# Cross-attention and spectral feed-forward on one core: GpSimd's and ScalarE's work of slots 7 to 12 in another order

## The chip, the cores and the metric

The kernel runs on one core of a Trainium2 chip. The metric is the device time of one execution in microseconds; three executions of the kernel before gave 442.58, 441.76 and 442.54. One further execution was recorded by the hardware profiler, and all rows below come from it.

The engines are TensorE (PE in the profile; PEld is its weight loads), VectorE (DVE), ScalarE (ACT), GpSimd (POOL) and the SP queue (SPq), which issues nearly all transfers. Every engine works through its own list of instructions in order, and they hand work to each other by semaphores.

## What is computed

Two residual layers on x (2 x 2048 rows of 512). This is the reference, cut to what matters:

```python
x = x + cross_attention(layernorm(x), ctx, mask)     # 16 heads of 32, 128 keys
x = x + real(ifft(fft(layernorm(x)) @ w)) + bias     # y = layernorm(x) @ M + bias

score = (q . k) / sqrt(32) * mask
score = where(score == 0, -1e9, score)               # the zero test
context = softmax(score) @ v ;  out = context @ wo + bo
```

## The kernel before

The 4096 rows are 16 blocks of 256 rows (c = 0 to 15), each of two tiles of 128 rows (t = 0, 1). Each block has four attention steps s = 4c to 4c + 3, one for four heads. `plan()` writes one order of slots v = 2 to 79 for all engines; every engine's program is a loop over v with what it has to do in that slot, written out by hand. Nothing is scheduled at run time: a wait at the head of an engine's list holds all behind it.

In slot v TensorE does: `turn` (L616) of step v - 2, 8 transposes of the exponentials in `zs`; a product of the middle kind (`WO` of block c - 2, tile 0 or 1, in slots 4c and 4c + 1; `FF` of block c - 3, tile 0 or 1, in slots 4c + 2 and 4c + 3; in slots 4 to 11 the eight products `U` and `M` that build the matrix M from the spectral weights); the scores of step v + 1 (L590); in odd slots `weigh` (L629), the weighted sum of values; then late products (`R`, `ST`, `QQ`). So WO(0, 0) is in slot 8, WO(0, 1) in 9, FF(0, 0) in 14, FF(0, 1) in 15, just ahead of the scores of step 16, the first step of block 4.

VectorE per step: `mask_mul` (L929), `zero_to_neg` (L936, the zero test), `least` (L941, the row minimum). GpSimd's `bias` (L1189) scales the minimum, and ScalarE's `exps` (L729) needs that. ScalarE's `copy_pt` (L738) copies the turned exponentials, which `weigh` needs; its `high_m` (L708) rounds a row block of M to 16 bits, VectorE's `low_m` (L920) makes the rest of it.

GpSimd also adds the output bias to the rows of x (`add_bo`, L1142), which the WO result is added to; makes the statistics' columns of a block (`stat_cols`, L1116, six small instructions); subtracts for the low half of the context (`ctx_lo`, L1202); spreads reciprocals (`spread`, L1196). From slot 4 on it waits in each slot for `eq_done`, that is until the zero test of that slot's step has ended, ahead of its long work.

After WO(c, t) the rows x1 are split into two 16-bit parts, `x1nh` (`norm_hi2`, L1154 on GpSimd for a few tiles, L716 on ScalarE for the others) and `x1nl` (`norm_lo2`, L1160, on GpSimd, which counts `p_l2`). The SP queue then turns both by DMA (`turn_x1n`, L372: two transposes, L385) into `x1h` and `x1l`, and FF(c, t) on TensorE waits for both (`d_t2`, L583). The order in which the SP queue issues, with its waits, is:

- slot 7: the query stack of block 3, then in slot 8 the mask and transposed rows of later blocks
- slot 11: `turn_x1n(0, 0)` (waits for `p_l2` of 1), `load_x(7)`, `stack_q(4)` (2 transfers of a row and 12 of `qh` and `ql`, L306: the operands of the scores of step 16)
- slot 12: `turn_x1n(0, 1)` (waits for `p_l2` of 2), `load_mask(5)`, `load_xt(7)`
- slot 15: `turn_x1n(1, 0)`, and so on

Per block there is only this one list, so block 0's second pair of transposes is behind the whole query stack of block 4.

Of the kernel before, what the change touches and what calls it, by code (L numbers as in the profile page):

```python
# [17 lines left out]
NC = NB * S // CH  # L18
NS = 4 * NC
# [98 lines left out]

def bo_slot(c):

    return c + 7 if c < 2 else 10 if c == 2 else 4 * c + 3 if c < 13 else 2 * c + 27


def build(nc, x, xt, ctx_in, mask, wq, bq, wk, bk, wv, bv, wo, bo, lparts, tables, bf, eye, sums, pick, places, heads, out):
# [3 lines left out]
    with ExitStack() as stack:  # L128
# [155 lines left out]
        def tile_of(c, t):  # L284
            return 2 * c + t

        def cast_count(n):

            return n + 1 - min(max(n + 1 - tile_of(12, 0), 0), 4)

        def columns(n):

# [370 lines left out]
        def _(act):  # L663
# [42 lines left out]
            def high_m(c):  # L706
                act.wait_ge(g_free, at["M", c] + 1)
                act.activation(mh[:, c, :], mf[:], ACT.Identity, scale=SO / D).then_inc(m_hi, 1)  # L708
# [82 lines left out]
            for v in range(V0, V1):  # L791
                c, r = divmod(v, 4)
                prompt, held, mids = slots[v][1:]
                if v % 2 == 1 and 0 <= v - 5 < NS - 2:
                    copy_rec((v - 5) // 2)
                for n in prompt:
                    hi(n)
                if v == 3:
                    hi(at["QQ", 2, 0])
                if 2 <= v - 1 < NS:  # L800
                    exps(v - 1, 0)
                if 3 < v < VQ:
                    for n in held:
                        hi(n)
                if 0 <= v - 2 < NS:
                    copy_pt(v - 2, 0)
                    copy_pt(v - 2, 1)
                if v == 2:
                    hi(at["ST", 2])
                    act.wait_ge(d_wo, 16)  # L810
                    act.activation(wos[:], wos[:], ACT.Identity, scale=SO).then_inc(w_sc, 1)
                    act.wait_ge(w_sc, 1)
                    act.copy(woh[:], wos[:]).then_inc(w_hi, 1)
                if v == 9:
                    high_m(0)
                if 2 <= v - 1 < NS:
                    exps(v - 1, 1)
                if v % 2 == 1 and 0 <= v - 5 < NS - 2:
                    ctx_hi((v - 5) // 2)
                if v == NS + 1:  # L820
                    copy_rec(NS // 2 - 1)
                if 1 <= v - 9 < 4:
                    high_m(v - 9)
                if v >= VQ:
                    for n in held:
                        hi(n)
                for n in mids:
                    if fills[n] != ("ST", 2):
                        hi(n)
                if v == 3:  # L830
                    split_hi(3)
                if r == 1 and 0 <= c - 2 < NC and v != NS + 1 and c - 2 not in (12, 13):
                    norm_hi2(c - 2, 0)
                if v == NS + 2:
                    norm_hi2(NC - 2, 0)
                    ctx_hi(NS // 2 - 1)
                if v == NS + 3:
                    norm_hi2(NC - 2, 1)
                if r == 2 and 0 <= c - 2 < NC and v != NS + 2 and c - 2 not in (12, 13):
                    norm_hi2(c - 2, 1)  # L840
                for a in range(4, NC):
                    if hi_slot(a) == v:
                        split_hi(a)
# [264 lines left out]
        def _(pool):  # L1108
# [45 lines left out]
            def norm_hi2(c, t):  # L1154
                n = tile_of(c, t)
                pool.wait_ge(g_free, at["WO", c, t] + 1)
                pool.wait_ge(d_t2[t], 32 * c)
                step(pool.tensor_copy(x1nh[:, t], x1[:, n % NO, :]))

            def norm_lo2(c, t):  # L1160
                n = tile_of(c, t)
                if c not in (12, 13):
                    pool.wait_ge(h2_done, cast_count(n))
                pool.tensor_tensor(x1nl[:, t], x1[:, n % NO, :], x1nh[:, t], ALU.subtract).then_inc(p_l2, 1)  # L1164

# [103 lines left out]
            for v in range(V0, V1):  # L1269
                c, r = divmod(v, 4)  # L1270
                if v == 8:
                    constant_row()
                for a in range(5, NC):
                    if small_slot(a) == v:
                        stat_cols(a)
                if v == NS + 1:
                    spread(NS // 2 - 1)
                if r == 1 and 0 <= c - 2 < NC and v != NS + 1:
                    rstd2(c - 2, 0)
                if v == NS + 2:  # L1280
                    rstd2(NC - 2, 0)
                    ctx_lo(NS // 2 - 1)
                if v == NS + 3:
                    rstd2(NC - 2, 1)
                if r == 2 and 0 <= c - 2 < NC and v != NS + 2:
                    rstd2(c - 2, 1)
                if VP <= v < NS:
                    pool.wait_ge(eq_done, v + 1)
                if v in (11, 12):
                    norm_lo2(0, v - 11)  # L1290
                if VT <= v < NS and r >= 2:
                    norm_lo2(c - 2, r - 2)
                if v == 4:
                    split_lo(3, slice(2, 4))
                if v == 5:
                    fold(9)
                if v == 6:
                    ctx_lo(0)
                for a in range(5, NC):
                    if v == 4 * a - 11:  # L1300
                        split_lo(a, slice(0, 2), False)
                    if v == 4 * a - 10:
                        split_lo(a, slice(2, 4))
                for a in range(3, 14):
                    if bo_slot(a) == v:
                        add_bo(a, 0)
                if v == 52:
                    add_bo(12, 1)
                if v == 56:
                    add_bo(13, 1)  # L1310
                if v == 60:
                    add_bo(14, 0)
                if v in (57, 61):
                    norm_hi2(c - 2, 0)
                if 0 <= v < NS:
                    bias(v)
                for n in {2: (4, 5), 4: (6, 7, 8), 5: (10, 11)}.get(v, ()):
                    fold(n)
                if v == 6:
                    split_lo(4)  # L1320
                    stat_cols(4)
                if v == 7:
                    scale_mask(2)
                if v == 9:
                    pool.wait_ge(m_lo, 1)
                if v == 10:
                    pool.wait_ge(m_lo, 2)
                if v % 2 == 1 and 2 <= v - 5 < NS - 2:
                    ctx_lo((v - 5) // 2)
                if r == 2 and 1 <= c - 2 < NC - 1 and not VT <= v < NS:  # L1330
                    norm_lo2(c - 2, 0)
                if r == 3 and 1 <= c - 2 < NC - 1 and not VT <= v < NS:
                    norm_lo2(c - 2, 1)
                if r < 2 and 0 <= c - 3 < NC and v > 12 and not (r == 1 and VT <= v < NS):
                    add_bf(c - 3, r)
                if r == 2 and VT <= v < NS:
                    add_bf(c - 3, 1)
                if v in (58, 62):
                    norm_hi2(c - 2, 1)
                if v == 60:  # L1340
                    add_bo(14, 1)
                if v == 3:
                    low_o(0)
                    spread(0)
                    low_o(1)
                if v == NS + 1:
                    add_bo(15, 0)
                if v == NS + 3:
                    add_bo(15, 1)
                if v == small_slot(3):  # L1350
                    stat_cols(3)
                for a in range(3):
                    if bo_slot(a) == v:
                        add_bo(a, 0)
                        add_bo(a, 1)
                for a in range(3, 12):
                    if bo_slot(a) == v:
                        add_bo(a, 1, slice(0, D // 2), False)
                    if bo_slot(a) + 3 == v:
                        add_bo(a, 1, slice(D // 2, D))  # L1360
                if v == 3:
                    split_lo(3, slice(0, 2), False)
                if v > VP and v % 2 == 1 and 0 <= v - 3 < NS - 2:
                    spread((v - 3) // 2)
                if r == 0 and 3 <= c + 1 < NC:
                    if v == 12:
                        add_bf(0, 0)
                    scale_mask(c + 1)

# [97 lines left out]
```

## Time and profile before

| what | value |
|---|---|
| median of the three runs | 442.54 us |
| the profiled execution | 441.81 us |
| its span, first to last instruction | 439.9 us |
| TensorE busy | 430.4 us, 98% |
| VectorE busy | 398.3 us, 91% |
| ScalarE busy | 366.1 us, 83% |
| GpSimd busy | 357.6 us, 81% |

Busy shares are means over a start-up of about 40 us, a regular middle part and an end; where the time goes is read from the order of the instructions on TensorE and from the idle time ahead of each. A number in square brackets at the end of a row of the timeline is the idle time just ahead of that row, and what ended it.

### The profile page before, as it was taken

The page shows a single profiled execution, that of the slowest core. Times are in us where ns is not written, and L with a number is a line of the kernel's source. Part 1 is how long each engine was busy: PE and PEld are TensorE (multiplying, and loading weights), DVE is VectorE, ACT ScalarE, POOL GpSimd, SP SyncE. Part 2 cuts the span into 40 slices and gives each one's busy share as a digit, 9 for nine tenths or more (in the row PEclk, how much of TensorE's full clock was granted, in tenths as well). Part 3 has the DMA queues.
Part 4 walks back from the last instruction along what each step waited for, and adds up shares of the span by engine and source line. Part 5 has one row for each costly group of instructions (what it writes and reads, how often), then busy time and mean ns, then how long its engine had stood idle before and what let it go on. Part 6 is the DMA issues. An engine that isn't in the chain of part 4 may idle for free.

```text
span 439.9 us, 10908 instructions
## 1 busy us (share of the span) xinstructions
PE 430.4 (98%) x3496; PEld 297.0 (68%) x3496; DVE 398.3 (91%) x532; ACT 366.1 (83%) x1338; POOL 357.6 (81%) x487
## 2 busy tenths in 40 slices
PE   7999999999999999999999999999999999999997
PEld 6887788676666776667677667766667675555544
DVE  2899899999999999999999999999999899999453
ACT  1668998899999899898989998999999899999710
POOL 5879889967979898989989898989898866676782
DMA  8999854404555455535455554455442334321144
GB/s 270 396 390 236 289 180 115 114 0 103 116 136 128 140 97 131 146 110 145 119 149 129 132 149 113 106 100 149 133 101 63 95 89 111 77 73 48 50 107 133
DMA packets 85286, 60.15 MB, mean 137 GB/s; under 512 B 40141, under 2 KB 72813, under 8 KB 84718
## 3 DMA queue, kind: packets, MB, share of 16 engines
q1 hardware_dynamic: 84508, 59.29, 49.6%
q8 instruction: 29, 0.48, 0.5%
q10 hardware_dynamic: 722, 0.17, 0.2%
q14 instruction: 27, 0.22, 0.2%
HBM read 29.33 MB, written 8.39 MB: 86 GB/s over the span
## 4 chain that ended last, share of the span: by engine, by line
PE 81%; DVE 9%; issue 3%; ACT 3%; POOL 3%; DVEq 0%; POOLq 0%
PE bank L467 31%; PE bank L472 22%; PE bank L626 10%; PE bank L640 6%; PE scores L612 5%; PE bank L573 2%; DVE zs L936 2%; PE bank L554 2%; DVE zs L929 2%; ACT zs L729 2%; PE scores L472 1%; PE bank L646 1%; ACT pt L738 1%; POOL cl L1202 1%; DVE cn L954 1%
## 5 line engine op out<-in xcount | busy, mean ns | idle before, releaser
L729 ACT ACTIVATE zs<-zs,nbias 128x128 f32<-128x128 f32 x512 | 199.6, 395 | 11.9 <-POOL nbias L1189 11.3
L729 ACT ACTIVATION_READ_ACCUMULATOR zs<-zs,nbias 128x1 f32 x512 | 98.6, 193 | 0.0
L936 DVE SCALAR_TENSOR_TENSOR zs<-zs 128x1024 f32<-128x1024 f32 x64 | 89.1, 1392 | 1.1
L941 DVE TENSOR_REDUCE nmin<-zs 128x8 f32<-128x1024 f32 x64 | 78.0, 1219 | 2.1
L929 DVE TENSOR_TENSOR zs<-scores,ms 128x1024 f32<-128x1024 f32 x64 | 78.0, 1218 | 0.1
L738 ACT COPY pt<-bank 128x512 f32<-128x512 f32 x128 | 67.8, 581 | 8.0 <-PE bank L626 7.9
L626 PE MATMUL bank<-ident,zs 128*128 128x128 f32 x512 | 67.1, 274 | 1.5 <-ACT zs L729 1.1
L1142 POOL TENSOR_TENSOR xs<-xs,bob 128x512 f32<-128x512 f32 (+1 forms) x41 | 42.3, 1036 | 24.9 <-DVE zs L936 23.5
L472 PE MATMUL bank<-xth,wqh 128*128 128x256 f16 x224 | 61.2, 273 | 0.0
L626 PEld LDWEIGHTS bank<-ident,zs 128*128 128x128 f32 x512 | 57.4, 140 | 5.4 <-ACT zs L729 4.3
L472 PE MATMUL bank<-xth,wql 128*128 128x256 f16 x224 | 61.1, 273 | 0.0
L472 PE MATMUL bank<-xtl,wqh 128*128 128x256 f16 x224 | 61.1, 273 | 0.0
L467 PE MATMUL bank<-woh,ch 128*128 128x512 f16 x128 | 48.5, 379 | 1.4 <-POOL cl L1202 1.4
L467 PE MATMUL bank<-woh,cl 128*128 128x512 f16 x128 | 48.5, 379 | 0.0
L467 PE MATMUL bank<-wol,ch 128*128 128x512 f16 x128 | 48.5, 379 | 0.0
L467 PE MATMUL bank<-mh,x1h 128*128 128x512 f16 x120 | 45.5, 379 | 0.0
L467 PE MATMUL bank<-ml,x1h 128*128 128x512 f16 x120 | 45.5, 379 | 0.0
L467 PE MATMUL bank<-mh,x1l 128*128 128x512 f16 x120 | 45.5, 379 | 0.0
L1196 POOL COPY rzb<-rz 128x512 f32<-128x512 f32 x32 | 41.6, 1299 | 3.8 <-DVE rz L947 3.7
L1164 POOL TENSOR_TENSOR x1nl<-x,x1nh 128x512 f16<-128x512 f32 x30 | 34.8, 1161 | 10.3 <-DVE zs L936 10.3
L612 PEld LDWEIGHTS scores<-ks,qs 102*128 102x128 f16 (+1 forms) x480 | 31.7, 98 | 14.6 <-DVE zs L929 1.6
L1175 POOL TENSOR_TENSOR x<-x,bfb 128x512 f32<-128x512 f32 x32 | 40.8, 1275 | 0.0
(126 smaller groups left out, 903.3 us busy)
## 6 DMA issues: line engine op xcount, KB each, us to landing
xs<-in_x SPq DMA_DIRECT2D x16, 512.0 KB, 4.4
xtr<-in_xt SPq DMA_DIRECT2D x16, 512.0 KB, 4.5
out<-x SPq DMA_DIRECT2D x31, 256.0 KB, 2.5
qs<-qh SPq DMA_DIRECT2D x120, 64.0 KB
lp<-in_lparts SPq DMA_DIRECT2D x4, 1024.0 KB, 10.5
qs<-ql SPq DMA_DIRECT2D x60, 64.0 KB
ms<-in_mask SPq DMA_DIRECT2D x16, 128.0 KB, 2.4
wks<-in_wk SPq DMA_DIRECT2D x2, 512.0 KB, 6.5
```

The source lines that it names most:

```text
L467: last = pe.matmul(o, a, b, start=(i == 0), stop=(i == len(mm) - 1))
L472: last = pe.matmul(o, a, b, start=(first and i == 0), stop=(i == len(pairs) - 1))
L612: last = pe.matmul(A[:, n % 2, 128 * j:128 * j + 128], qs[c % 2][0:rows, g, j, 128 * t:128 * t + 128], ks[0:rows, g, j, c // (NC // NB), : ...
L626: last = pe.transpose(PB[f][:, a:a + 128], zs[:, s % NZ, t, 2 * f + i, :], ident[:])
L729: last = act.activation(z, z, ACT.Exp, bias=nbias[:, s % 4, i:i + 1], scale=-NEG, accum_out=zsum[:, s % 4, i:i + 1])
L738: act.copy(pt[:, s % 2, 2 * f:2 * f + 2, :], PB[f][:]).then_inc(pt_copied, 1)
L929: dve.tensor_tensor(zs[:, s % NZ], A[:].rearrange("p t (h k) -> p t h k", h=4), ms[:, c % NM].unsqueeze(2).broadcast_to([128, 2, 4, KEYS]) ...
L936: dve.scalar_tensor_tensor(out=z, in0=z, scalar=0.0, in1=z, op0=ALU.is_equal, op1=ALU.subtract).then_inc(eq_done, 1)
L941: dve.tensor_reduce(nmin[:, s % 4, :], zs[:, s % NZ].rearrange("p t h k -> p (t h) k"), AX.X, ALU.min).then_inc(mn_done, 1)
L1142: i = pool.tensor_tensor(z, z, bob[:, n], ALU.add)
L1175: pool.tensor_tensor(z, z, bfb[:], ALU.add).then_inc(p_x1b, 1)
L1196: pool.tensor_copy(rzb[:].rearrange("p i h w -> p (i h) w"), rz[:, z, :].rearrange("p i h -> p (i h)").unsqueeze(2).broadcast_to([128, 16, ...
```

## The change

Only GpSimd's and ScalarE's lists change; the lists of TensorE, VectorE and the SP queue are the same instruction for instruction. In words:

- `add_bo` of block 0 leaves slot 7 for slot 8, behind the wait for the zero test of step 8 (its first half ahead of `bias(8)`, its second behind). `add_bo` of block 1 is split over slots 8 and 10, that of block 2 over slots 11 and 14. `stat_cols(5)` comes behind `bias(8)`.
- The high halves of block 0's rows are cast on GpSimd (in slots 9 and 10) and no longer on ScalarE. The low halves, `norm_lo2(0, 0)` and `norm_lo2(0, 1)`, which were in slots 11 and 12 ahead of `bias(11)` and `bias(12)`, both stand at the end of slot 12's list.
- In slot 11 GpSimd also waits for `m_lo` of 3 behind `bias(11)`.
- ScalarE takes the first exponentials of step 8 in slot 8, those of steps 9 and 10 at the head of slots 10 and 11, the second ones of step 9 ahead of `copy_pt`, and the matrix rows (`high_m`) 1, 2 and 3 earlier in their slots.

The core of the diff, ScalarE's loop first:

```diff
+                if v in (10, 11):
+                    exps(v - 1, 0)
...
-                if 2 <= v - 1 < NS:
+                if 2 <= v - 1 < NS and v not in (9, 10, 11):
                     exps(v - 1, 0)
+                if v == 10:
+                    exps(v - 1, 1)
+                    high_m(1)
+                if v == 12:
+                    high_m(3)
...
-                if 2 <= v - 1 < NS:
+                if v == 11:
+                    high_m(2)
+                    hi(at["M", 3])
+                if 2 <= v - 1 < NS and v != 10:
                     exps(v - 1, 1)
+                if v == 8:
+                    exps(v, 0)
...
-                if 1 <= v - 9 < 4:
-                    high_m(v - 9)
...
-                if r == 1 and 0 <= c - 2 < NC and v != NS + 1 and c - 2 not in (12, 13):
+                if r == 1 and 0 <= c - 2 < NC and v != NS + 1 and c - 2 not in (0, 12, 13):
                     norm_hi2(c - 2, 0)
```

GpSimd's loop:

```diff
-                if v in (11, 12):
-                    norm_lo2(0, v - 11)
+                if v == 8:
+                    add_bo(0, 0)
...
+                if v == 8:
+                    add_bo(0, 1)
+                    stat_cols(5)
+                    add_bo(1, 0)
                 if v == 9:
                     pool.wait_ge(m_lo, 1)
+                    norm_hi2(0, 0)
                 if v == 10:
                     pool.wait_ge(m_lo, 2)
+                    norm_hi2(0, 1)
+                    add_bo(1, 1)
+                if v == 11:
+                    pool.wait_ge(m_lo, 3)
...
                     if v == 12:
+                        norm_lo2(0, 0)
+                        norm_lo2(0, 1)
                         add_bf(0, 0)
                     scale_mask(c + 1)
```

GpSimd's order from slot 7 to the middle of slot 8, before. The names: `cl` is the low context, `xs` the rows that get the output bias, `rzb` the spread reciprocals, `ve` to `rs` the start of the statistics' columns, `nbias` the scaled minimum of step 8 behind its wait for the zero test.

```order
L1202 TENSOR_TENSOR cl<-cn,ch 128x512
L1142 TENSOR_TENSOR xs<-xs,bob 128x512 x2
L1196 COPY rzb<-rz 128x512
L1226 MEMSET tb 1x256
L1119 TENSOR_SCALAR ve_98<-ag_97 128x2
L1122 TENSOR_TENSOR rs_99<-ve_98,half 128x2
```

The same place after the change:

```order
L1213 TENSOR_TENSOR cl<-cn,ch 128x512
L1207 COPY rzb<-rz 128x512
L1237 MEMSET tb 1x256
L1152 TENSOR_TENSOR xs<-xs,bob 128x512
L1200 TENSOR_SCALAR nbias<-nmin 128x8
L1152 TENSOR_TENSOR xs<-xs,bob 128x512
```

The two additions to `xs` moved from ahead of the zero test of step 8 to behind it.

GpSimd's order over slots 11 and 12, before, from `norm_lo2(0, 0)` (the first row) to `norm_lo2(0, 1)` (the row ahead of the last); the statistics' columns in the middle are those of block 6, and the last row is `bias(12)`.

```order
L1164 TENSOR_TENSOR x1nl<-x_76,x1nh 128x512
L1189 TENSOR_SCALAR nbias<-nmin 128x8
L1202 TENSOR_TENSOR cl<-cn,ch 128x512
L1196 COPY rzb<-rz 128x512
L1119 TENSOR_SCALAR ve_98<-ag_97 128x2
L1122 TENSOR_TENSOR rs_99<-ve_98,half 128x2
L1123 TENSOR_TENSOR ag_97<-ve_98,half 128x2
L1124 CAST h_100<-ag_97 128x4
L1128 COPY stok<-h_100 128x2x2x2
L1129 TENSOR_TENSOR stok<-ag_97,h_100 128x2x2
L1164 TENSOR_TENSOR x1nl<-x_76,x1nh 128x512
L1189 TENSOR_SCALAR nbias<-nmin 128x8
```

After the change, from `bias(11)` on:

```order
L1200 TENSOR_SCALAR nbias<-nmin 128x8
L1213 TENSOR_TENSOR cl<-cn,ch 128x512
L1152 TENSOR_TENSOR xs<-xs,bob 128x256
L1207 COPY rzb<-rz 128x512
L1129 TENSOR_SCALAR ve_98<-ag_97 128x2
L1132 TENSOR_TENSOR rs_99<-ve_98,half 128x2
L1133 TENSOR_TENSOR ag_97<-ve_98,half 128x2
L1134 CAST h_100<-ag_97 128x4
L1138 COPY stok<-h_100 128x2x2x2
L1139 TENSOR_TENSOR stok<-ag_97,h_100 128x2x2
L1200 TENSOR_SCALAR nbias<-nmin 128x8
L1175 TENSOR_TENSOR x1nl<-x_76,x1nh 128x512 x2
```

Both subtractions for `x1nl`, on which the transposes of the SP queue wait, moved behind `bias(12)`.

## Rows read from the trace of the kernel before

**Rows 1.** The page, its first line of busy times.
```profile
PE 430.4 (98%) x3496; PEld 297.0 (68%) x3496; DVE 398.3 (91%) x532; ACT 366.1 (83%) x1338; POOL 357.6 (81%) x487
```
**Rows 2.** Timeline of TensorE, slots 10 to 13 (start, us, what [idle]).
```profile
92.37 1.89 PE L472 MATMUL bank<-tb,us 128*128 128x256 f32 x8
94.10 0.61 PE L612 MATMUL scores<-ks,qs 102*128 102x128 f16 x8
...
95.86 1.89 PE L472 MATMUL bank<-tb,us 128*128 128x256 f32 x8
98.08 0.62 PE L612 MATMUL scores<-ks,qs 102*128 102x128 f16 x8 [0.32 <-DVE zs L929]
99.12 1.07 PE L640 MATMUL bank<-pt,vs 128*32 128x256 f32 x16 [0.42 <-ACT pt L738]
...
111.44 0.62 PE L612 MATMUL scores<-ks,qs 102*128 102x128 f16 x8 [0.40 <-DVE zs L929]
```
**Rows 3.** Timeline of VectorE, slots 8, 10 to 12, and block 7's statistics.
```profile
76.02 2.30 DVE L936 SCALAR_TENSOR_TENSOR zs<-zs 128x1024 f32<-128x1024 f32 x1
...
96.13 0.76 DVE L871 TENSOR_TENSOR mf<-bank,od 128x256 f32<-128x256 f32 x2
...
101.69 1.32 DVE L920 SCALAR_TENSOR_TENSOR ml<-mf,mh 128x512 f16<-128x512 f32 x1 [0.67 <-ACT mh L708]
...
103.94 1.16 DVE L929 TENSOR_TENSOR zs<-scores,ms 128x1024 f32<-128x1024 f32 x1
...
106.40 1.22 DVE L941 TENSOR_REDUCE nmin<-zs 128x8 f32<-128x1024 f32 x1
...
120.86 0.68 DVE L968 BATCH_NORM_STATS2 st<-xs 128x6 f32<-128x512 f32 x1
```
**Rows 4.** Timeline of the SP queue, slots 11 and 12.
```profile
101.03 1.33 SPq L385 DMA_TRANSPOSE x1h<-x1nh  x1
...
105.89 0.64 SPq L306 DMA_DIRECT2D qs<-qh  x1
...
113.94 1.28 SPq L385 DMA_TRANSPOSE x1h<-x1nh  x1
115.26 2.39 SPq L385 DMA_TRANSPOSE x1l<-x1nl  x1
```
**Rows 5.** The tile x1l, from 113.5 to 118 us: from issue to landing.
```profile
DMA to landing us min/median/max: 3.5/3.5/3.5
```
**Rows 6.** Timeline of TensorE, slots 14 and 15.
```profile
116.71 0.38 PE L467 MATMUL bank<-mh,x1h 128*128 128x512 f16 x1
...
121.07 0.38 PE L467 MATMUL bank<-mh,x1h 128*128 128x512 f16 x1
...
123.66 0.61 PE L612 MATMUL scores<-ks,qs 102*128 102x128 f16 x8
```
**Rows 7.** Timeline of ScalarE, slot 10: the copy for matrix row block 2.
```profile
95.20 0.36 ACT L684 COPY od<-bank 128x256 f32<-128x256 f32 x1
```
**Rows 8.** Timeline of GpSimd, slots 7, 8, 11 and 12.
```profile
77.19 1.60 POOL L1196 COPY rzb<-rz 128x512 f32<-128x512 f32 x1
...
79.02 0.22 POOL L1119 TENSOR_SCALAR ve<-ag 128x2 f32<-128x2 f32 x1
...
81.46 0.26 POOL L1189 TENSOR_SCALAR nbias<-nmin 128x8 f32<-128x8 f32 x1
...
101.30 1.16 POOL L1202 TENSOR_TENSOR cl<-cn,ch 128x512 f16<-128x512 f32 x1
...
104.09 0.61 POOL L1196 COPY rzb<-rz 128x512 f32<-128x512 f32 x1 [1.63 <-DVE rz L947]
...
107.67 1.16 POOL L1164 TENSOR_TENSOR x1nl<-x,x1nh 128x512 f16<-128x512 f32 x1
```
**Rows 9.** Timeline of TensorE, its first matmuls.
```profile
2.28 3.17 PE L646 MATMUL bank<-qh 128*128 128x256 f16 x14 [2.28 <-POOL srow L1246]
...
6.43 1.26 PE L646 MATMUL bank<-qh 128*128 128x256 f16 x10
```

More of the change, by code:

```diff
@@ L119, in bo_slot @@
 def bo_slot(c):
-    return c + 7 if c < 2 else 10 if c == 2 else 4 * c + 3 if c < 13 else 2 * c + 27
+    return 4 * c + 3 if c < 13 else 2 * c + 27
 def build(nc, x, xt, ctx_in, mask, wq, bq, wk, bk, wv, bv, wo, bo, lparts, tables, bf, eye, sums, pick, places, heads, out):
@@ L287, in cast_count @@
         def cast_count(n):
-            return n + 1 - min(max(n + 1 - tile_of(12, 0), 0), 4)
+            return n + 1 - min(n + 1, 2) - min(max(n + 1 - tile_of(12, 0), 0), 4)
         def columns(n):
@@ L827, in _ @@
                 for n in mids:
-                    if fills[n] != ("ST", 2):
+                    if fills[n] not in (("ST", 2), ("M", 3)):
                         hi(n)
@@ L838, in _ @@
                     norm_hi2(NC - 2, 1)
-                if r == 2 and 0 <= c - 2 < NC and v != NS + 2 and c - 2 not in (12, 13):
+                if r == 2 and 0 <= c - 2 < NC and v != NS + 2 and c - 2 not in (0, 12, 13):
                     norm_hi2(c - 2, 1)
@@ L1156, in norm_hi2 @@
                 pool.wait_ge(g_free, at["WO", c, t] + 1)
-                pool.wait_ge(d_t2[t], 32 * c)
+                if c >= 1:
+                    pool.wait_ge(d_t2[t], 32 * c)
                 step(pool.tensor_copy(x1nh[:, t], x1[:, n % NO, :]))
@@ L1161, in norm_lo2 @@
                 n = tile_of(c, t)
-                if c not in (12, 13):
+                if c not in (0, 12, 13):
                     pool.wait_ge(h2_done, cast_count(n))
@@ L1272, in _ @@
                     constant_row()
-                for a in range(5, NC):
+                for a in range(6, NC):
                     if small_slot(a) == v:
@@ L1303, in _ @@
                         split_lo(a, slice(2, 4))
-                for a in range(3, 14):
+                for a in range(2, 14):
                     if bo_slot(a) == v:
@@ L1351, in _ @@
                     stat_cols(3)
[L1352 to L1356, printed above, removed]
+                for a in range(2, 12):
                     if bo_slot(a) == v:
```

## The prediction

> **What bounds the kernel now.** I read the page first. TensorE is busy 98% of the span [rows 1], so anything this change can give must come from places where TensorE waits, and anything that makes it wait anew is lost. Next the timeline of TensorE, start by start: from slot 14 to slot 55 its instructions follow each other without a gap, so a shift of TensorE in slots 10 to 15 goes through to the end as it is. The only gaps of slots 4 to 13 that the profile shows are three: the scores of step 12 (0.32 us, for VectorE), the weighted sum behind them (0.42, for ScalarE's copy) and the scores of step 14 (0.40, for VectorE) [rows 2]. Ends of matmuls are modelled, so starts tell more: the same eight matmuls for M take 94.10 - 92.37 = 1.73 us to the next start when nothing waits and 98.08 - 95.86 = 2.22 where they do, 0.49 and not 0.32 [rows 2]. With 0.17 more for each of the three, the gaps are 1.14 + 0.51 = **about 1.6 us**. That is all that can be won there.
>
> Then the engines behind these gaps. VectorE's zero test of step 8 took 2.30 us beside GpSimd's additions; the chain that follows ends at M's low rows, which wait 0.67 us for ScalarE and then take 1.32 [rows 3]. Last, the SP queue: after idling since slot 8 (the waits view names GpSimd's x1nl as what it waited for) it issues from 101.03 on without a pause, the transposes of rows (0, 0), x of block 7, the query stack of block 4 from 105.89, and the transposes of rows (0, 1) at 113.94 and 115.26 [rows 4]. The last lands 3.5 us after its issue [rows 5], at 118.76. FF(0, 1) starts at 121.07 [rows 6]. So it has a margin of 2.3 us, and the whole train hangs on the moment at which GpSimd finishes `x1nl` of tile (0, 0).
>
> **The gain.** Without GpSimd's additions beside it the zero test of step 8 should take the 1.2 us that VectorE's neighbours of that size take; that is up to 1.08 us [rows 3]. The same additions come back behind the test, 2.5 us on GpSimd either way, ahead of and behind `bias(8)`, and they cost TensorE nothing, because WO(0, 0) reaches VectorE later. With matrix rows 1 and 2 rounded sooner on ScalarE, the wait of 0.67 and the long form of 1.32 (0.64 over the usual 0.68) go too [rows 3]. What is late next on VectorE is the third product for M, which TensorE ends as the scores of step 11 start, 94.10 [rows 2]: a hand-over of some 0.2 us and ScalarE's copy of 0.36 [rows 7] put VectorE's subtraction at 94.7 and not 96.13 [rows 3]. From there to `mask_mul(12)` VectorE needed 103.94 - 96.13 = 7.81 us, less 0.67 and 0.64 is 6.50, so 101.2; from the start of `mask_mul(12)` to the end of `least(12)` it is 106.40 + 1.22 - 103.94 = 3.68 [rows 3], so 104.9. VectorE is then 2.7 us earlier than before, more than the gaps were, and all 1.6 us are won up to slot 14. That GpSimd casts `x1nh` (and ScalarE does not) hides in ScalarE's and GpSimd's slack; it adds two short instructions to GpSimd and has no reader sooner than `norm_lo2`.
>
> **The loss.** `norm_lo2(0, 0)` was ahead of `bias(11)`; now it is behind `bias(12)`. What is ahead of it on GpSimd and cannot be passed: `bias(12)` needs `least(12)`, 104.9 at the best. The list itself is later still. `ctx_lo(3)` now waits for M's low row block 2 and for ScalarE's context copy; by the walk above the first is done near 100.3, and before it began at 101.30 [rows 8], so I take 100.6. Then 1.16 for it [rows 8], about 0.65 for half an addition to `xs` (half of an addition of 1.25), the spread of reciprocals at 0.61 when alone to 1.60 when it runs beside a zero test, the statistics' columns of block 6 at 81.46 - 79.02 = 2.44, `bias(12)` at 0.26 and the subtraction at 1.16 [rows 8]: 6.28 to 7.27 us, so 106.9 to 107.9. I take **107.5** for the end of x1nl(0, 0), before it was 101.0: 6.5 us later. Because `spread(4)` now starts near 102.4, just where the zero test of step 12 does, I lean to the upper half.
>
> The Trainium skill bears on this: GPSIMD Engine Reference, its specification table, says that GpSimd shares its interfaces to SBUF with VectorE and contends with VectorE's instructions that have two SBUF inputs. By it the zero test, which reads `zs` twice, contends and `mask_mul`, which reads the scores from PSUM, does not; 2.30 against 1.22 us for the zero test agrees, and it would put the subtraction's end at 107.9 rather than 106.9.
>
> From there the SP queue repeats what it did: from its start at 101.03 to the landing of the last transpose of (0, 1) it took 118.76 - 101.03 = 17.73 us [rows 4, 5], issue bound, with 12 head transfers at some 0.65 us each. FF(0, 1) can start at 107.5 + 17.7 = **125.2**, where it started at 121.07 [rows 6]: **4.1 us later**. The 1.6 us won before do not help, since TensorE only reaches its wait sooner: it stands at 119.5 and waits 5.7 us. Everything on TensorE behind is dense, so the 4.1 us stay to the end.
>
> The other transfers that this start moves are covered. The transposes for FF(0, 0) are issued by 107.5 + 2.6 and land near 112.7, FF(0, 0) comes at 116.71 - 1.6 = 115.1 [rows 6]. x of block 7 goes out ahead of the first head transfer, so by 112.4, and its first reader on VectorE is at 120.86 [rows 3]. The query stack of block 4 ends its issue at 120.4; the scores of step 16, 2.6 us behind FF(0, 1) [rows 6], are at 127.8. The mask of block 5 and the transposed rows of block 7 go out near 124, at 117.7 before, for slot 16, which itself is 4 us later. For the next block the queue is 2 to 3 us late at most and TensorE 4 us, so this is paid once.
>
> **TensorE's clock.** The kernel's first 14 matmuls of 256 columns take 3.17 us together, the ten at 6.43 take 1.26 [rows 9]: starts 0.22 us apart and 0.11, the lower level of 1.2 GHz and the upper one of 2.4 GHz; the first came after idleness, the second after work. (The granted clock in the profile's columns says 1.00 throughout, so the durations are the better witness.) No row shows what an idle time of 5.7 us in mid-kernel does; the longest wait after the start is under 1 us. The bounds are nothing and, from the start, 13 x 0.11 = 1.5 us once more, with the products behind FF(0, 1) at half speed for some 3 us. I take 1.5, as the only idle time of more than 2 us that the trace has was followed by the lower level.
>
> The Trainium skill says the same for an idle engine, in TensorE: Matmul & The Clock Gate, Part 1: the half rate is the resting state, entered when TensorE idles, and released only by a stretch of work. No run here yet shows it for a pause inside the kernel.
>
> The sum, on the profiled execution's own 441.81 us (span 439.9 and 1.9 around it): 441.81 + 4.1 + 1.5 = **447.4 us**. The median of the runs, 442.54, lies 0.7 above that execution; I leave that difference to the range.
>
> **The rivals.** First, the same chain with the clock held through the wait: 441.81 + 4.1 = 445.9. For it: the wait is short and all else is dense.
> Second, the faster side: the SP chain is not what FF(0, 1) waits for, because `x1nl` of (0, 0) is done in time. It decides at 121.07 - 17.73 = 103.3: for an end of the subtraction up to there (less the 1.6 won, 101.7, for the whole gain) nothing is late and the time is 441.81 - 1.6 = 440.2. Against it: `least(12)` would have to end 3 us before what VectorE's own durations allow. It could also come true if the head transfers were issued faster than 0.65 us; no row of the SP queue shows that.
> Third, the change doesn't do what it says: VectorE does not get earlier, because GpSimd's new casts and additions meet other zero tests. Then `least(12)` ends at 107.6 as before, the subtraction at 109.1, FF(0, 1) at 126.8: 441.81 + 5.8 + 1.5 = 449.1.
> Fourth, no change: some gain elsewhere that just cancels a shorter delay, 441.8. I see no row for it.
>
> **How the numbers follow.** The forecast (delay and clock) 0.42, the clock held 0.31, VectorE not earlier 0.12, faster 0.09, no change 0.04, and 0.02 for a much worse time. The range takes in the ends of the subtraction's time (106.3 to 107.9, so a delay of 2.9 to 4.5) with and without the clock's part, and the third rival without its last half microsecond or so: 444.3 to 449.3. A measurement of this kernel can tell about 0.2% (0.9 us) from no change. Faster by more than that 0.09, within 0.04, slower 0.87.
>
> **What the profile after would show.** Right: a zero test of step 8 near 1.2 us; no waits of TensorE at the scores of steps 12 and 14; the SP queue idle until about 107.5 and then a train of the same length; one wait of 5 to 6 us ahead of FF(0, 1), ended by a transfer; matmuls twice as long behind it if the clock falls; dense TensorE later. Wrong: FF(0, 1) at or ahead of 121, or the train shorter than 17 us. If the wait is there and the matmuls behind it keep their pace, the clock's term was wrong.

## The result

| | before | after |
|---|---|---|
| median | 442.18 us (441.76 to 442.58, 4 runs) | 448.19 us (447.60 to 449.31, 4 runs) |
| ratio of after to before | | 1.0137, 95% interval 1.0119 to 1.0154 |
| span of the profiled execution | 439.9 us | 447.5 us |
| mean granted clock of TensorE | 1.000 | 0.992 |

The change costs 6.0 us at the medians, 1.4%; 447.4 had been forecast. The profiled execution of after is the slowest of its four; part of its 7.6 us more of span is the start. The two executions are set against each other at the first of the products U (L472, `bank<-tb,lp`), which no edit has touched: it starts at 50.89 us before and at 51.65 after, 0.76 us later. TensorE's first eight transposes, on which nothing of the change bears, show where that comes from, first before, then after:

```profile
5.53 1.06 PE L494 MATMUL bank<-ident,cxs 128*128 128x128 f32 x8
```

```profile
5.41 1.94 PE L494 MATMUL bank<-ident,cxs 128*128 128x128 f32 x8
```

In this execution TensorE kept its lower pace longer at the start. Of the rest, span less that start, 389.0 us became 395.8: **6.8 us** belong to the change.

### The profile page after: what moved, and what is told of

Read it like the earlier page. It is cut to its first block, busy times and chain, and to the rows that moved or that the text cites. A ratio compares the mean times of both kernels' runs of the same rounds, so it can differ in the third digit from the quotient of the medians.

```text
span 447.5 us, 10911 instructions
## 1 busy us (share of the span) xinstructions
PE 433.4 (97%) x3496; PEld 298.7 (67%) x3496; DVE 397.4 (89%) x532; ACT 364.7 (82%) x1336; POOL 357.0 (80%) x490
## 4 chain that ended last, share of the span: by engine, by line
PE 60%; DVE 6%; POOL 3%; issue 3%; ACT 1%; DMA 1%; SPq 0%; DVEq 0%; POOLq 0%
PE bank L467 30%; PE bank L472 12%; PE bank L626 8%; PE bank L640 5%; PE scores L612 4%; PE bank L573 2%; DVE zs L946 2%; DVE zs L939 1%; ACT zs L729 1%; POOL x L1186 1%; POOL cl L1213 1%; DVE cn L964 1%; DVE st L1008 1%; DVE x L918 1%; DVE x L924 1%
## 5 line engine op out<-in xcount | busy, mean ns | idle before, releaser
L1152 POOL TENSOR_TENSOR xs<-xs,bob 128x512 f32<-128x512 f32 (+1 forms) x42 | 43.6, 1038 | 31.2 <-DVE zs L946 31.2
L472 PE MATMUL bank<-xth,wqh 128*128 128x256 f16 x224 | 61.2, 273 | 0.0
L472 PE MATMUL bank<-xtl,wqh 128*128 128x256 f16 x224 | 61.1, 273 | 0.0
L472 PE MATMUL bank<-xth,wql 128*128 128x256 f16 x224 | 61.1, 273 | 0.0
L467 PE MATMUL bank<-mh,x1h 128*128 128x512 f16 x120 | 46.5, 387 | 5.5 <-DMA x1l<-x1nl 5.5
L467 PE MATMUL bank<-ml,x1h 128*128 128x512 f16 x120 | 46.4, 387 | 0.0
L1186 POOL TENSOR_TENSOR x<-x,bfb 128x512 f32<-128x512 f32 x32 | 41.7, 1306 | 0.0
L612 PEld LDWEIGHTS scores<-ks,qs 102*128 102x128 f16 (+1 forms) x480 | 31.9, 97 | 13.5 <-issue 0.4
L1213 POOL TENSOR_TENSOR cl<-cn,ch 128x512 f16<-128x512 f32 x32 | 37.1, 1158 | 3.4 <-ACT ch L752 3.2
```

The costliest lines, as they stand in the source:

```text
L467: last = pe.matmul(o, a, b, start=(i == 0), stop=(i == len(mm) - 1))
L472: last = pe.matmul(o, a, b, start=(first and i == 0), stop=(i == len(pairs) - 1))
L612: last = pe.matmul(A[:, n % 2, 128 * j:128 * j + 128], qs[c % 2][0:rows, g, j, 128 * t:128 * t + 128], ks[0:rows, g, j, c // (NC // NB), : ...
L1152: i = pool.tensor_tensor(z, z, bob[:, n], ALU.add)
L1186: pool.tensor_tensor(z, z, bfb[:], ALU.add).then_inc(p_x1b, 1)
L1213: pool.tensor_tensor(cl[:, c % 2, 2 * h:2 * h + 2, :], cn[:], ch[:, c % 2, 2 * h:2 * h + 2, :], ALU.subtract).then_inc(p_cl, 1)
```

## The profile after

The timeline of TensorE in slots 11 to 15 (start, us, what, [idle time and what ended it]). It answers [rows 2] and [rows 6]:

```profile
98.37 0.61 PE L612 MATMUL scores<-ks,qs 102*128 102x128 f16 x8
98.91 1.07 PE L640 MATMUL bank<-pt,vs 128*32 128x256 f32 x16
...
110.48 0.61 PE L612 MATMUL scores<-ks,qs 102*128 102x128 f16 x8
...
118.12 0.61 PE L612 MATMUL scores<-ks,qs 102*128 102x128 f16 x8
119.44 0.63 PE L573 MATMUL bank<-ident,rzb 128*128 128x128 f32 x4 [0.71 <-POOL rzb L1207]
119.90 1.04 PE L626 MATMUL bank<-ident,zs 128*128 128x128 f32 x8
126.43 0.58 PE L467 MATMUL bank<-mh,x1h 128*128 128x512 f16 x1 [5.49 <-DMA x1l<-x1nl]
126.81 0.63 PE L467 MATMUL bank<-ml,x1h 128*128 128x512 f16 x1
127.23 0.63 PE L467 MATMUL bank<-mh,x1l 128*128 128x512 f16 x1
...
131.02 0.38 PE L467 MATMUL bank<-mh,x1l 128*128 128x512 f16 x1
131.24 0.61 PE L612 MATMUL scores<-ks,qs 102*128 102x128 f16 x8
```

Four things are to be seen. The three waits of slots 10 to 13 are gone: the scores of step 14 start at 110.48 and not 111.44, though the start-up was 0.76 later. A new wait of 0.71 stands in slot 14, for GpSimd's spread of reciprocals. FF(0, 1) waits 5.49 us, and what ended it was the landing of the transposed low half. And behind it the matmuls stand 0.43 us apart where they stood 0.22; the scores of step 16 come 4.81 us after FF(0, 1)'s start, 2.59 before [rows 6].

The SP queue, which answers [rows 4]:

```profile
108.99 1.32 SPq L385 DMA_TRANSPOSE x1h<-x1nh  x1
110.36 1.25 SPq L385 DMA_TRANSPOSE x1l<-x1nl  x1
111.66 0.59 SPq L350 DMA_DIRECT2D xs<-in_x  x1
...
122.44 1.30 SPq L385 DMA_TRANSPOSE x1h<-x1nh  x1
123.77 1.26 SPq L385 DMA_TRANSPOSE x1l<-x1nl  x1
```

It is the train of before, 8 us later. From its first transposition to FF(0, 1) it is 126.43 - 108.99 = 17.44 us. And GpSimd, of slots 11 and 12, which answers [rows 8]:

```profile
100.69 0.65 POOL L1200 TENSOR_SCALAR nbias<-nmin 128x8 f32<-128x8 f32 x1
101.41 1.16 POOL L1213 TENSOR_TENSOR cl<-cn,ch 128x512 f16<-128x512 f32 x1
102.53 0.74 POOL L1152 TENSOR_TENSOR xs<-xs,bob 128x256 f32<-128x256 f32 x1
103.21 0.61 POOL L1207 COPY rzb<-rz 128x512 f32<-128x512 f32 x1
103.79 1.19 POOL L1129 TENSOR_SCALAR ve<-ag 128x2 f32<-128x2 f32 x1
...
107.21 0.26 POOL L1200 TENSOR_SCALAR nbias<-nmin 128x8 f32<-128x8 f32 x1
107.43 2.65 POOL L1175 TENSOR_TENSOR x1nl<-x,x1nh 128x512 f16<-128x512 f32 x2
```

The clock, in the view by stretches of 2 us. The columns are the length, the busy time of TensorE, its weight loads, VectorE, ScalarE and GpSimd with their counts, the granted clock, the DMA share and GB/s:

```profile
122.00:124.00 2.00, 0.00 (x0) 0.00 (x0) 1.34 (x2) 0.00 (x0) 1.38 (x2) 1.00 0.46 104
124.00:126.00 2.00, 0.00 (x0) 0.00 (x0) 0.00 (x0) 0.00 (x0) 0.00 (x0) 0.53 0.51 104
126.00:128.00 2.00, 1.57 (x4) 0.58 (x5) 0.50 (x1) 1.63 (x5) 0.00 (x0) 0.50 0.66 123
128.00:130.00 2.00, 2.00 (x6) 0.73 (x5) 1.97 (x3) 2.00 (x9) 0.58 (x1) 0.50 1.09 324
130.00:132.00 2.00, 2.00 (x16) 0.98 (x18) 1.15 (x2) 2.00 (x9) 0.91 (x2) 0.76 0.78 178
```

TensorE has nothing to do from about 121 on, the clock goes to half (1.2 of 2.4 GHz) while it idles, and comes back after some 4 us of work. The second row shows nothing on any engine: all of them stood behind one transfer.

The balance of TensorE by its starts (each start-to-start against the same pair of instructions elsewhere in the trace): before, the waits of slots 10 to 13 are 0.49, 0.50, 0.19, 0.56 and 0.22, together 1.96 us. After they are gone, and there are 0.87 (spread), 5.66 (transposes) and 2.22 (slow matmuls), together 8.75. The difference is 6.8 us, as above.

## Experiments

Ten further runs. "From U" is the span less the start of the first product U in the profiled execution; it takes out the start-up, which differed by up to 2.8 us between executions.

| run | median us | ratio to before, interval | from U |
|---|---|---|---|
| before | 442.18 | | 389.0 |
| the change | 448.19 | 1.0137 (1.0119 to 1.0154) | 395.8 |
| e1, low halves back | 441.74 | 0.9990 (0.9974 to 1.0006) | 388.6 |
| e2, low halves alone | 450.32 | 1.0185 (1.0160 to 1.0210) | 397.4 |
| e3, stack issued first | 441.57 | 0.9986 (0.9975 to 0.9996) | 388.6 |
| e4, filler matmuls | 447.53 | 1.0125 (1.0098 to 1.0152) | 393.9 |
| e5, one low half forward | 442.58 | 1.0011 (1.0002 to 1.0020) | 389.6 |
| e6, e3 and spread sooner | 441.45 | 0.9984 (0.9975 to 0.9993) | 388.5 |
| e7, the change again | 448.16 | 1.0142 (1.0125 to 1.0160) | 395.4 |
| e8, filler again | 447.67 | 1.0123 (1.0106 to 1.0140) | 394.2 |
| e9, e6 and bias(13) sooner | 441.75 | 0.9994 (0.9982 to 1.0006) | 388.4 |
| e10, zero test alone | 442.09 | 1.0008 (0.9994 to 1.0022) | 389.1 |

**The theory.** The loss is one mechanism: `norm_lo2(0, 0)` behind `bias(12)`, hence the SP queue's train late, hence FF(0, 1), hence the clock. The rest of the change is a gain. The rival: the other moves cost too.

### e1: the low halves back at their places

```diff
+                if v in (11, 12):
+                    norm_lo2(0, v - 11)
                 if v == 8:
                     add_bo(0, 0)
...
                     if v == 12:
-                        norm_lo2(0, 0)
-                        norm_lo2(0, 1)
                         add_bf(0, 0)
```

> The change, with the two low halves of block 0's rows (x1nl) back at their old places, ahead of bias(11) and bias(12). Theory (the loss is the SP queue's train behind x1nl(0,0), the rest of the change is a gain of some 1.7 us): about 440.5 us, 0.996 of the kernel before, SP queue's transposes at about 101.5, no wait of TensorE ahead of FF(0,1). Rival (the other moves of GpSimd and ScalarE cost time themselves): 444 us or more.

441.74 us: the whole loss is gone, and no wait stands ahead of FF(0, 1). The rival falls. But 440.5 it is not: waits of 0.30, 0.48 and 0.67 us by starts (slots 12 to 13) have come in place of the 1.96. From U the gain is 0.4 us, and at the medians it can't be told from nothing.

### e2: nothing but the low halves moved

```diff
-                if v in (11, 12):
-                    norm_lo2(0, v - 11)
...
                     if v == 12:
+                        norm_lo2(0, 0)
+                        norm_lo2(0, 1)
                         add_bf(0, 0)
```

> The kernel before, with only the two low halves of block 0's rows moved to the end of slot 12's list. Theory: GpSimd ends x1nl(0,0) near 109.1, the train of 17.4 us ends at 126.6, FF(0,1) is 5.5 us later and TensorE's clock costs 2.2 more: about 450 us. Rival (the other moves cost): 442 to 444 us.

450.32 us. The SP queue of this run starts its transposes later still than in the change:

```profile
109.65 1.32 SPq L385 DMA_TRANSPOSE x1h<-x1nh  x1
...
124.78 1.26 SPq L385 DMA_TRANSPOSE x1l<-x1nl  x1
```

and TensorE starts FF(0, 1) 17.8 us after it, with the same kind of row:

```profile
127.42 0.59 PE L467 MATMUL bank<-mh,x1h 128*128 128x512 f16 x1 [5.39 <-DMA x1l<-x1nl]
```

So the move alone makes the whole loss, and without the rest of the change 2.1 us more at the medians, 1.6 from U.

### e3: the query stack ahead of the transposes

The change, in which the SP queue issues `load_x(7)` and `stack_q(4)` ahead of `turn_x1n(0, 0)`:

```diff
+                if v == 11:
+                    load_x(7)
+                    stack_q(4)
                 if r == 3 and 0 <= c - 2 < NC - 1:
                     turn_x1n(c - 2, 0)
```

> The change, with the SP queue's list in another order at slot 11: x of block 7 and the query stack of block 4 are issued ahead of the transposes of tile (0,0), all else as in the change. Theory: the stack goes out near 95.5 to 105, both pairs of transposes near 109 to 114, the last lands by 117, ahead of FF(0,1)'s turn at 120.8: no wait, about 440.5 us, 0.996 of before. Rival (FF(0,1) is late for GpSimd's lateness itself or for transfers as such, not for the queue's order): still 445 us or more.

GpSimd is just as late here, but the queue is not:

```profile
94.92 1.42 SPq L337 DMA_DIRECT2D qs<-srow  x2
...
104.36 0.82 SPq L306 DMA_DIRECT2D qs<-qh  x1
108.40 1.32 SPq L385 DMA_TRANSPOSE x1h<-x1nh  x1
109.78 1.25 SPq L385 DMA_TRANSPOSE x1l<-x1nl  x1
111.07 1.26 SPq L385 DMA_TRANSPOSE x1h<-x1nh  x1
112.38 1.27 SPq L385 DMA_TRANSPOSE x1l<-x1nl  x1
```

The stack fills the time in which the queue stood idle, the second pair of transposes is issued 2.7 us behind the first instead of 13.5, and FF(0, 1) waits for nothing. 441.57 us: it is the order of the queue that carries GpSimd's lateness to TensorE. This is faster than the kernel before, but by 0.14% only, and 1.1 us short of the 440.5 that was expected. Left on TensorE by its starts: 0.88 in slot 14 (GpSimd's spread), 0.28 in slot 15, 0.19 in slot 17.

### e4 and e8: filler matmuls in the wait, and e7 beside e8

```diff
                     pe.wait_ge(m_lo, 4)
+                    if (c, f) == (0, 1):
+                        for i in range(48):
+                            pe.matmul(o[:, 0:256], wqh[:, 0, 0:128], woh[:, 0, 0:256], start=True, stop=True)
```

> The change, with 48 matmuls of 256 columns (5.2 us at full rate, results overwritten) put ahead of FF(0,1)'s wait for its transposes, so that TensorE works through most of that wait. Theory (idleness of TensorE lowers its clock and costs 2.2 us behind the wait): FF(0,1) starts as before near 126.4, its matmuls 0.216 us apart, granted clock 1.00, about 446.0 us. Rival (the slow matmuls come from something else, such as transfers beside them): matmuls 0.43 us apart, 448.2 us.

> The change with 48 matmuls of 256 columns ahead of FF(0,1)'s wait, again, beside the change itself on one chip. Theory (idleness lowers the clock): 2.0 us less than the change, 446.2 us against 448.2, matmuls 0.216 us apart. Rival (the clock's part shows in the trace but the time doesn't follow, since other waits take its place): within 0.7 us of the change.

> The change as it is, again, on the same chip as the run with filler matmuls: about 448.2 us, a wait of 5.5 us ahead of FF(0,1), its matmuls 0.43 us apart, granted clock 0.99.

In e4 the fillers take the place of the wait and the clock holds (e4: TensorE's timeline, then the stretch in which the change had half the clock):

```profile
120.35 5.42 PE L585 MATMUL bank<-woh,wqh 128*128 128x256 f16 x48
125.67 0.39 PE L467 MATMUL bank<-mh,x1h 128*128 128x512 f16 x1
125.89 0.38 PE L467 MATMUL bank<-ml,x1h 128*128 128x512 f16 x1
...
129.35 1.07 PE L643 MATMUL bank<-pt,vs 128*32 128x256 f32 x16 [0.47 <-ACT pt L741]
```

```profile
126.00:128.00 2.00, 2.00 (x11) 0.88 (x9) 1.17 (x2) 2.00 (x9) 0.00 (x0) 1.00 0.83 214
```

So the slow matmuls came from idleness, and not from the transfers beside them. That agrees with the Trainium skill, TensorE: Matmul & The Clock Gate, Part 1, by which half rate is the resting state of an idle engine and work releases it. The time followed only in part. On one chip the change had 448.16 us and the filler 447.67, where the theory had said 446.2; the rival's "within 0.7 us of the change" is what came. From U the two profiles of the change have 395.8 and 395.4, those with filler 393.9 and 394.2, 1.2 to 1.9 us less. But 0.3 us of that lies ahead of FF(0, 1), where no slow matmul is: from U to its start it is 74.8 us in both profiles of the change and 74.5 in both with filler. From FF(0, 1)'s start to the end of the span it is 321.1 and 320.6 against 319.4 and 319.8, so 0.8 to 1.6 us less. Some of what the clock cost is given back at once: TensorE, back at its pace, meets ScalarE's copy at the weighted sum (the last row of the timeline, 0.47), which the slow matmuls had hidden. Start-ups differ by 0.6 us between the two profiled executions on that chip, as much as the 0.5 us by which the medians differ. So the clock's mechanism is shown, and its price stays open between 0.5 us (medians) and 1.6.

The price also differs from execution to execution of one kernel. In e7 only about 9 of FF(0, 1)'s 12 matmuls were slow and the next scores came 4.35 us after its start (4.81 in the first profile of the change, 5.05 in e2); the four executions of e7 had mean clocks of 0.992, 0.996, 0.992 and 0.996.

### e5: one low half forward

The change with `norm_lo2(0, 0)` alone moved from the end of slot 12 to behind `ctx_lo(3)` in slot 11.

> The change, with the low half of tile (0,0) alone moved forward, behind ctx_lo(3) in slot 11, where it ends near 103.3 to 103.8; that of (0,1) stays at the end of slot 12. Theory (FF(0,1) starts 17.4 us after that end, or at its turn): 120.7 to 121.2 against a turn of 120.8 to 121.7, so a wait of 0 to 0.5 us, clock kept, 441.5 to 442.0 us (the short waits seen in the two runs without the train come in its place). Rival (the lateness of tile (0,1)'s own half counts too): a wait of 2 us or more ahead of FF(0,1), 443.5 us or more.

The train starts at 103.75, 5.2 us sooner than in the change, and the wait shrinks to

```profile
121.95 0.38 PE L467 MATMUL bank<-mh,x1h 128*128 128x512 f16 x1 [1.31 <-DMA x1l<-x1nl]
```

with the clock held. 442.58 us, 0.6 above the expected range. The wait is 0.8 us more than the 0.5 at most that was expected, and less than the rival's 2, since the train took 18.2 us and not 17.4. Where the 0.8 come from is read from its end:

```profile
115.34 1.31 SPq L306 DMA_DIRECT2D qs<-ql  x1
...
117.35 1.28 SPq L385 DMA_TRANSPOSE x1h<-x1nh  x1
118.68 1.26 SPq L385 DMA_TRANSPOSE x1l<-x1nl  x1
```

The view of `x1l`, 118.5 to 120 us, from the issue of the last transpose to its landing:

```profile
DMA to landing us min/median/max: 3.1/3.1/3.1
```

The issue is not what made it longer: from the first transpose to the last it is 118.68 - 103.75 = 14.93 us here and 123.77 - 108.99 = 14.78 in the change, though one transfer of `ql` took 1.31 us here. The last transpose landed 3.1 us after its issue where the same view gives 2.5 in the change. `x1nl` of tile (0, 1) was done long before 118.68, so its own lateness does not count. Why a landing takes 3.1 us here, 2.5 in the change and 3.5 before was not tried.

### e6 and e9: what eats the gain

With the train out of the way 1.6 us should have been won and 0.5 were. e6 is e3 with `spread(5)` ahead of `add_bf(0, 1)` in slot 13; e9 is e6 with `add_bf(0, 0)` moved behind `bias(13)`:

```diff
+                if v == 13:
+                    spread(5)
+                    add_bf(0, 0)
                 if r < 2 and 0 <= c - 3 < NC and v > 12 and not (r == 1 and VT <= v < NS):
                     add_bf(c - 3, r)
...
                     if v == 12:
                         norm_lo2(0, 0)
                         norm_lo2(0, 1)
-                        add_bf(0, 0)
```

> The change, with the SP queue's order of the run that issued block 4's query stack first, and with GpSimd's spread(5) put ahead of the bias addition to tile (0,1) in slot 13. Theory (what is left of the change's gain after the train is gone was lost to GpSimd's full list: 0.9 us where TensorE waited for that spread): the wait at the transposes of reciprocals in slot 14 goes from 0.72 us to none, 440.7 us, 0.997 of before. Rival (another wait takes its place in slot 14 or 15): 441.5 us as without it.

> The run with the query stack first and spread(5) sooner, and with the bias addition to tile (0,0) moved from the end of slot 12's list to behind bias(13), in slot 13. Theory (what still eats the gain is that GpSimd's slot 12 list is too long, so bias(13) comes late and ScalarE waits 1.8 us for it): that wait falls to about 0.5 us, the wait of TensorE at the turn of step 13 (0.6 by its starts) goes, the time from the first product U to the end of the span falls from 388.5 to about 387.7 us, 440.7 us in all, 0.997 of before. Rival (the wait moves on to another instruction): as without it, 441.4 us.

Both times the wait that was named went and another took its place. In e6 TensorE passes the spread and waits for step 13's exponentials, because ScalarE had waited for `bias(13)`:

```profile
117.87 0.61 PE L576 MATMUL bank<-ident,rzb 128*128 128x128 f32 x4
118.92 1.09 PE L629 MATMUL bank<-ident,zs 128*128 128x128 f32 x8 [0.44 <-ACT zs L732]
```

```profile
114.72 0.40 ACT L732 ACTIVATE zs<-zs,nbias 128x128 f32<-128x128 f32 x1 [1.80 <-POOL nbias L1203]
```

In e9 ScalarE's wait for `bias(13)` falls to 0.62, as expected, and TensorE waits a slot later, for ScalarE's copy ahead of the weighted sum:

```profile
124.23 0.64 PE L643 MATMUL bank<-pt,vs 128*32 128x256 f32 x8 [1.21 <-ACT pt L741]
```

That copy stands behind step 14's first exponentials in ScalarE's list, and these now wait for `bias(14)`, 1.79 us where it was 0.60 in e6, since the addition was moved ahead of it:

```profile
121.58 0.40 ACT L732 ACTIVATE zs<-zs,nbias 128x128 f32<-128x128 f32 x1 [1.79 <-POOL nbias L1203]
```

441.45 and 441.75 us, and from U 388.6, 388.5 and 388.4 for e3, e6 and e9: no difference that can be told. The rivals were right in both. What e9 does show is where the load sits: GpSimd works without a pause in slots 12 to 14, and moving a piece of its list moved the wait to another slot.

### e10: the zero test by itself

The kernel before with only the additions of block 0 moved behind the zero test of step 8.

> The kernel before, with only the bias additions of block 0 moved behind the zero test of step 8 (one ahead of bias(8), one behind). Theory (VectorE's whole chain was late by that test): the test takes 1.23 us and not 2.30, the waits of TensorE in slots 10 to 13, 1.96 us by its starts, shrink to about 1 us, 441.2 us. Rival (the additions only meet something else, and what waits is the matrix rows on ScalarE): the test is short but the waits stay, 442.2 us.

The test takes 1.23 us instead of the 2.30 of [rows 3], and nothing comes of it: 442.09 us, as the rival said. VectorE's timeline shows where the time went:

```profile
76.45 1.23 DVE L936 SCALAR_TENSOR_TENSOR zs<-zs 128x1024 f32<-128x1024 f32 x1
...
95.77 0.69 DVE L920 SCALAR_TENSOR_TENSOR ml<-mf,mh 128x512 f16<-128x512 f32 x1 [1.00 <-ACT mh L708]
...
102.11 1.33 DVE L920 SCALAR_TENSOR_TENSOR ml<-mf,mh 128x512 f16<-128x512 f32 x1 [0.66 <-ACT mh L708]
```

VectorE arrives sooner and waits 1.00 for ScalarE's matrix row (`mh`), where it waited 0.32 before. TensorE's waits are those of before, 0.49, 0.50, 0.20, 0.56 and 0.22 by starts. So the zero test alone wins none of the 1.96 us. What the traces point to is ScalarE's new order: in the change `mh` of row blocks 1 and 2 starts at 92.56 and 98.31 where it started at 94.68 and 101.01, and VectorE no longer waits for it. In e1, which has that order too, the 0.99 us of the scores of step 12 and of the weighted sum behind them are gone, while others of slots 12 and 13 are back, so these hang on where GpSimd has its subtractions. ScalarE's new order alone, without the other moves, was not tried; that it carries the gain is argued and not shown.

## Why the prediction was right, point by point

- **The gaps to be won.** 1.6 us were counted, 1.96 were there by starts (five waits, two of which the profile's idle column does not name), all gone after. Right in kind. The working gave the zero test of step 8 a part in it; e10 shows that this part alone is worth nothing.
- **What the gain meets next.** The prediction said that additions and casts would be hidden on GpSimd. They were not quite: the wait of 0.87 us for the spread in slot 14 is new, and e3, e6 and e9 show that GpSimd's full list leaves 0.5 us of the gain. This step was missed; in the change the long wait behind it covers it.
- **The end of x1nl(0, 0).** Forecast 107.5 in the time frame of before. The transposes started at 108.99, less the 0.76 of start-up 108.2. `ctx_lo(3)` began where it was put (101.41 - 0.76 = 100.65); from there to the transposes' start it was 7.58 us against 6.28 to 7.27, so even the upper end was 0.3 short. The spread took its 0.61 us and not 1.60. The excess is in the statistics' columns, 107.21 - 103.79 = 3.42 us for 2.44, where the first small one took 1.19 instead of 0.22, and in the two subtractions, 2.65 for 2.3. The first lay beside the zero test of step 12, which took 1.52 us instead of 1.22; that of step 13 took 1.96 beside the operations that follow the subtractions. That agrees with the sentence of the Trainium skill (GPSIMD Engine Reference, 1. Specifications) on VectorE instructions with two SBUF inputs. No run took the two apart, so that the one slows the other is read from their standing side by side.
- **The train.** 17.7 us forecast, 17.44 measured, 17.4 to 18.2 over all runs that waited for it. Two parts cancel in it: from the first transpose's issue to the last's it was 14.78 us and not 14.23, and the last landed 2.5 us after its issue and not 3.5.
- **The start of FF(0, 1).** 4.1 us later forecast; 126.43 - 0.76 - 121.07 = 4.6 measured. The wait was 5.7 by the forecast, 5.66 by starts; that these agree so well is luck, since the later start (0.5) and the larger gain (0.4) are made up for by the wait for the spread (0.9), which the forecast did not have.
- **The clock.** 1.5 us by the matmuls of the start (13 x 0.11 is 1.43); 2.22 by starts in the profile, 1.8 in e7, and 0.8 to 1.6 in the traces when it is taken away by filler. The start-up was the right witness for the kind. It was short for the pace, since the slow stretch behind FF(0, 1)'s start lasted over 4 us and not 3, and near for the time, since the term left out that the slow matmuls hide a later wait; that 1.5 lies between 0.8 and 1.6 is in part luck.
- **The sum.** 5.6 us forecast, 6.8 in the aligned profiles (6.4 with e7's), 6.0 at the medians. The mechanism came as it was told; delay and clock were each somewhat larger in the trace. The third rival (VectorE not earlier) is what e2 builds: 450.3 against its 449.1.
- **The faster rival** decided at an end of x1nl(0, 0) of 103.3; e5 ends it at 103.7, 103.0 when its start-up is taken off, and is not faster but 0.1% slower (1.0011, 1.0002 to 1.0020), for its longer train and its other waits for GpSimd and ScalarE.

## What to carry to other kernels

A transfer queue that issues in order turns one late operand into the lateness of everything listed behind it; when an operation is moved, look up who waits for it on the queue, and add the whole train (here 17 us) to the new end. Where the queue idles ahead of such a wait, work that is ready belongs ahead of it, as in e3. And when an engine is named as late, look what it waits for next before paying: the zero test was 1.07 us too long and worth nothing, because VectorE waited for ScalarE a few instructions later anyway.

## What the runs showed of the hardware

- TensorE's granted clock went from 1.00 to 0.50 inside an idle time of 5.5 us in mid-kernel, in every profile with that wait (the change, e2, e7), and held through waits of 1.3 us and less (e5, e9) and through filler work (e4, e8). How long the slow stretch lasted differed, also between executions of one kernel: about 9 (e7), 11 (the change) and all (e2) of the 12 matmuls behind it were slow. At the start too: the same eight transposes took 1.06 us in one execution and 1.94 in another.
- At the start of the kernel the view says 1.00 where the first matmuls of 256 columns stand 0.22 us apart and soon after 0.11 [rows 9]; in mid-kernel it says 0.50 where those of 512 columns stand 0.43 us apart and not 0.22. Durations tell the clock also where the column does not.
- One order of 14 transfers on the SP queue took between 9.5 us (before) and 10.4 (e2) to issue (from the first `srow` transfer to the end of the last `qh`), with single issues of 0.8 to 1.7 us among those of 0.60.
- A DMA transpose issued at the end of such an order landed 2.5 us after its issue in the change, e2, e4, e7 and e8, 3.1 in e5, 3.5 before and 4.0 in e1.
